# Delta attention on one core: the joins of neighbouring waves' inverses put side by side, and one transfer for their blocks

## What is computed

```python
mixed = (hidden_states @ W_qkvz).reshape(b, s, 16, 2*128 + 2*2*128)   # q, k, v, z of 16 key heads, 2 value heads each
qkv_c = silu(causal_conv4(q | k | v))
g = -exp(A_log) * softplus(a + dt_bias); beta = sigmoid(b_gate)
# by chunks of each value head
decay = exp(tril(g_cum_i - g_cum_j))
L = -(k * beta) @ k.T * decay, strictly lower
attn = solve_triangular(eye - L, eye, lower=True)                     # an inverse of a unit triangle
# the chain over a head's chunks
v_new = attn-solved v - attn-solved k @ state
out_i = (q * exp(g)) @ state + (q @ k.T * decay) @ v_new
state = state * exp(g_last) + (k * exp(g_last - g)).T @ v_new
# behind it
xf = core * silu(z); xf = xf * rsqrt(mean(xf * xf) + 1e-6) * norm_weight
out = xf @ W_out
```

## Time and profile before

| | |
|---|---|
| median of three executions | 2001.9 us |
| the profiled execution | 2008.92 us, span 2008.9 us |
| PE busy, loads of its weights | 1827.1 us (91%), 1171.5 us |
| DVE busy | 1353.0 us (67%) |
| ACT busy | 1041.1 us (52%) |
| POOL busy | 1018.1 us (51%) |

### The profile page before, as it was taken

How to read it: one execution, slowest core, us unless ns; L and a number is a source line. 1 busy time by engine, 2 the same in 40 slices (tenths; PEclk the granted TensorE clock), 3 DMA queues, 4 the chain that set the end, 5 groups by cost and what they waited for, 6 DMA issues and landing times.

```text
span 2008.9 us, 46738 instructions
## 1 busy us (share of the span) xinstructions
PE 1827.1 (91%) x16855; PEld 1171.5 (58%) x16855; DVE 1353.0 (67%) x2827; ACT 1041.1 (52%) x2817; POOL 1018.1 (51%) x2259
## 2 busy tenths in 40 slices
PE   7799997877799886898999999999999999999987
PEld 6422564432244565345677767776777677677766
DVE  2544464595669433636887888887778778888853
ACT  2466232224421342525666766766666677667653
POOL 0531122233100241124777877777777777777772
PEclk7899999897999796899999999999999999999988
DMA  5035423110010633202222222222222222222221
GB/s 138 21 98 176 105 46 54 55 65 1 1 45 0 172 117 102 35 20 51 53 51 63 62 47 63 65 53 54 65 65 55 54 65 65 55 54 65 49 41 32
DMA packets 231187, 124.48 MB, mean 62 GB/s; under 512 B 141360, under 2 KB 210512, under 8 KB 230704
## 3 DMA queue, kind: packets, MB, share of 16 engines
q1 hardware_dynamic: 225008, 111.20, 22.5%
q0 software_dynamic: 5952, 10.29, 2.3%
HBM read 87.94 MB, written 39.74 MB: 64 GB/s over the span
## 4 chain that ended last, share of the span: by engine, by line
PE 38%; DVE 6%; POOL 4%; ACT 4%; issue 3%; SPq 3%; DMA 2%; DVEq 0%; POOLq 0%; ACTq 0%
PE ps L2054 9%; PE ps L2064 4%; PE ps L2264 4%; PE ps L2231 3%; DVE a_qkv L2673 3%; PE ps L2240 2%; PE ps L2212 2%; PE ps L2295 2%; POOL a_z L2645 2%; POOL a_term L2641 2%; PE ps L2100 1%; SPq L1987 1%; PE ps L2199 1%; DVE a_low L2690 1%; PE ps L2251 1%
## 5 line engine op out<-in xcount | busy, mean ns | idle before, releaser
L2645 POOL TENSOR_TENSOR a_z<-a_z,a_term 32x14 f32<-32x14 f32 (+6 forms) x896 | 308.8, 345 | 70.2
L2641 POOL TENSOR_TENSOR a_term<-a_z,a_l 32x14 f32<-32x14 f32 (+6 forms) x896 | 296.1, 330 | 70.3
L2673 DVE SCALAR_TENSOR_TENSOR a_qkv<-a_raw,a_taps,a_qkv 128x512 f32<-128x512 f32 x384 | 277.3, 777 | 1.4
L2054 PE MATMUL ps<-all_xn,a_w_qkv 128*128 128x512 f32 x512 | 247.9, 610 | 0.0
L2264 PE MATMUL ps<-a_out_t,a_w_out 128*128 128x256 f32 x512 | 131.8, 402 | 6.3 <-ACT a_out_t L2510 5.7
L2408 ACT ACTIVATE a_raw<-ps 128x512 f32<-128x512 f32 x128 | 76.1, 596 | 108.7 <-PE ps L2054 108.6
L2635 POOL COPY a_z<-a_l 32x256 f32<-32x256 f32 x64 | 34.2, 535 | 189.9 <-DMA a_l<-a_v_dram 189.7
L2054 PEld LDWEIGHTS ps<-all_xn,a_w_qkv 128*128 128x128 f32 x512 | 89.4, 193 | 69.4 <-issue 67.5
L390 POOL DMA_INDIRECT f_rows<-a_row,a_slots x32 | 35.4, 1105 | 184.5 <-DVE a_of_tile L380 139.1
L2064 PE MATMUL ps<-a_w_z,all_xn 128*128 128x256 f32 x512 | 122.6, 383 | 0.0
L2264 PEld LDWEIGHTS ps<-a_out_t,a_w_out 128*128 128x128 f32 x512 | 94.7, 195 | 23.2 <-ACT a_out_t L2510 8.5
(11 more groups left out here) (343 smaller groups left out, 4417.0 us busy)
## 6 DMA issues: line engine op xcount, KB each, us to landing
a_gc_rows<-a_g_dram SPq DMA_DIRECT2D x64, 256.0 KB, 4.8
a_v_dram<-a_v SPq DMA_DIRECT2D x64, 256.0 KB, 2.1
a_w<-in_f_w SPq DMA_DIRECT2D x24, 512.0 KB, 4.4
a_w_qkv<-in_a_w SPq DMA_DIRECT2D x16, 512.0 KB
a_t_dram<-a_z SPq DMA_DIRECT2D x512, 8.0 KB
a_w_z<-in_a_w SPq DMA_DIRECT2D x16, 256.0 KB, 2.9
a_w_out<-in_a_wo SPq DMA_DIRECT2D x16, 256.0 KB, 3.1
a_v_off<-a_v SPq DMA_DIRECT2D x256, 4.0 KB
```

The lines of the kernel that those rows point to most:

```text
L2054: mm = pe.matmul(ps[:, to, :], w_qkv[:, k, mt * P:(mt + 1) * P], xn[:, k, b * T:(b + 1) * T], start=k == 0, stop=k == KC - 1)
L2641: pool.tensor_tensor(term[:, 0:j, j + 1:], z[:, 0:j, j:j + 1].broadcast_to([HP, j, n]), rows[:, j:j + 1, j + 1:].broadcast_to([HP, j, n]), ...
L2645: pool.tensor_tensor(z[:, 0:j, j + 1:], z[:, 0:j, j + 1:], term[:, 0:j, j + 1:], ALU.add).then_inc(sub_step, 1)
L2673: step = dve.scalar_tensor_tensor(to, rows, tap, to, ALU.mult, ALU.add)
```

## The change

1. **PE's order.** A round is now `join_a(w), close_b(w-1), make_scores(w+2), part 0, turn_keys(w+2), close_a(w), join_c(w-1), part 1, turn_out(w-2), join_b(w), close_c(w-1), recall(w-1)`, (c = 1: part 2), `project_out(w-2), solve(w-1)`, (c = 1: part 3, else part 2), `ask(w-1), grow_state(w-1), answer(w-1), turn_values(w+3)`; where c = 0, `turn_values` stands ahead of `ask`. The upper levels of wave w - 1 are now done in round w.
2. **The other engines' orders** follow: ACT's and DVE's loops are written anew, the exponents and `make_low` are made for w + 3 instead of w + 2 and `make_values` for w + 3, `widen` for w + 1. In the rounds c = 2 the convolutions go by batch (`conv_row`) between other steps. v0, v_far have a fourth buffer, `v0_off` two instead of three.
3. **SP.** The eight stores of a wave's inverted blocks become one of 32 partitions with 2 KB each; `z16` and `t_dram` are laid out for it, and the load that follows takes 128 bytes from four places for each partition. `spread` and `gather` are cut into five functions, whose order is the store of v0, the store of the blocks, the loads of `l16`, the load of the blocks, and the loads of `v0_off`.
4. **POOL** does `root(w-2), normed(w-2), substitute(w+2)`, which is the same order from wave to wave. `reduce` on DVE is gone: 1/128 goes into the scale of ACT's square, and the addition of 1e-6 is an instruction of POOL of 128x4 elements in `root`.
5. A constant tile `ident16` that nothing read is no longer loaded.

```diff
-                for w in range(-2, W + 1):
+                for w in range(-2, W + 2):
+                    if made(w - 2):
+                        root(w - 2)
+                        normed(w - 2)
                     if made(w + 2):
                         substitute(w + 2)
-                    if made(w - 1):
-                        root(w - 1)
-                        normed(w - 1)
...
                 def root(w):
-                    pool.wait_ge(var_ready, w + 1)
+                    pool.wait_ge(sq_ready, PR * (w + 1))
                     if w >= 1:
                         pool.wait_ge(xnorm_ready, w)
+                    pool.tensor_scalar(var[:, :], sums[:, :], 1e-6, None, ALU.add).then_inc(var_ready, 1)
+                    pool.wait_ge(var_ready, w + 1)
...
-                    if made(w + 3):
-                        load_gates(w + 3)
+                    if made(w + 4):
+                        load_gates(w + 4)
                     if made(w + 2):
-                        spread(w + 2)
+                        store_v0(w + 2)
                     if made(w + 1):
-                        gather(w + 1)
+                        store_t(w + 1)
+                    if made(w + 2):
+                        load_blocks(w + 2)
+                    if made(w + 1):
+                        load_t(w + 1)
+                    if made(w + 2):
+                        load_off(w + 2)
...
+                def store_t(w):
+                    sp.wait_ge(sub_done, w + 1)
+                    sp.dma_start(t_dram[w % 2].rearrange("(p x) -> p x", p=HP),
+                                 z16[:, w % 2, :, :, :].rearrange("p j k c -> p (j k c)")).then_inc(t_stored, 16)
...
                 for w in range(W + 2):
                     c, g = w % CH, w // CH + 1
                     silus = c == 1 and g < KH
                     if made(w - 1):
                         copy_half(w - 1)
                         copy_top(w - 1)
                         copy_far(w - 1)
                     if made(w - 2):
                         square(w - 2)
                     part(w, 0)
                     if made(w):
                         copy_tb(w)
                     if made(w - 1):
                         copy_wc(w - 1)
                     if silus:
                         silu(g, 0)
                     elif made(w + 2):
                         make_keys(w + 2)
                     if made(w - 2):
                         copy_out(w - 2)
                     if silus:
                         silu(g, 1)
                     if made(w):
                         copy_wb(w)
                     if made(w - 1):
                         copy_corners(w - 1)
                     part(w, 1)
                     if silus:
                         silu(g, 2)
                         part(w, 2)
                     else:
                         exponents(w + 3)
                     if made(w - 1):
                         new_values(w - 1)
                     if silus:
                         silu(g, 3)
                         part(w, 3)
                         exponents(w + 3)
                     else:
                         part(w, 2)
                     if made(w + 3):
                         make_values(w + 3)
```

More of the change, by code:

```diff
@@ L2344, in _ @@
                 f_lower(4)
+                turn_values(2)
                 for n in range(4):
@@ L2363, in _ @@
                 for w in range(W + 2):
[L2364 to L2374 removed]
+                    c = w % CH
                     if made(w):
@@ L2377, in _ @@
                     if made(w - 1):
-                        grow_state(w - 1)
+                        close_b(w - 1)
+                    if made(w + 2):
+                        make_scores(w + 2)
+                    part(w, 0)
+                    if made(w + 2):
+                        turn_keys(w + 2)
                     if made(w):
@@ L2381, in _ @@
                     if made(w - 1):
-                        answer(w - 1)
+                        join_c(w - 1)
+                    part(w, 1)
+                    if made(w - 2):
+                        turn_out(w - 2)
                     if made(w):
                         join_b(w)
-                    part(w, 1)
-                    if made(w):
-                        close_b(w)
-                    if made(w - 2):
-                        turn_out(w - 2)
-                    part(w, 2)
-                    if made(w + 2):
-                        turn_keys(w + 2)
-                    if made(w):
-                        join_c(w)
+                    if made(w - 1):
+                        close_c(w - 1)
+                        recall(w - 1)
+                    if c == 1:
+                        part(w, 2)
                     if made(w - 2):
                         project_out(w - 2)
-                    part(w, 3)
-                    if made(w):
-                        close_c(w)
+                    if made(w - 1):
+                        solve(w - 1)
+                    if c == 1:
+                        part(w, 3)
+                    else:
+                        part(w, 2)
+                    if c == 0 and made(w + 3):
+                        turn_values(w + 3)
+                    if made(w - 1):
+                        ask(w - 1)
+                        grow_state(w - 1)
+                        answer(w - 1)
+                    if c != 0 and made(w + 3):
+                        turn_values(w + 3)
             @block.scalar
@@ L2909, in _ @@
[L2909 to L2920 removed]
+                    if c == 2:
+                        conv_row(w, 1, 0)
+                    if made(w - 2):
+                        add_out(w - 2)
```

288 lines of the change are left out of this document (151 added, 137 removed).

## The result

| | before | after |
|---|---|---|
| median, us | 2004.9 (4 runs, 2001.8 to 2008.9) | 2134.6 (4 runs, 2124.0 to 2144.3) |
| ratio | 1 | **1.0635, 95% interval 1.0606 to 1.0663** |
| span of the profiled execution, us | 2008.9 | 2130.7 |
| granted clock, mean over the span | 0.952 | 0.918 |
| PE busy, us | 1827 | 1856 |

The change is slower by 6.3%, outside the range that was given.

What follows compares the result with a forecast made beforehand. PE was taken as the bound, with POOL next once PE gave 5%. PE's work, `turn_out` waits and ACT's delay summed to 67.35 us a head against 68.15, hence 1991 us against 2001.9; range 1964 to 2032.

Steps and rivals of the forecast that it cites:

- What the change takes off PE: On PE, fewer entries into and exits from tiled groups and small groups joined together: 2.5 us a head saved.
- The open term: On PE, eight changes from 32x32 to 64x64 tiles, shown by no row: between free and 0.19 us each.
- the lower bound: On PE, a full 0.19 us at each of the eight tile-size changes, leaving a saving of 1.0 us a head.
- The wait at c=1: PE at `turn_out` waits for POOL's xnorm about 3.4 us in each round c=1; 3.2 when carried from round to round.
- The chain: From v0 through store, block loads, `substitute`, `root` and `normed` on POOL: xnorm ready 20.6 us behind v0.
- The sum: Per head: PE's work 62.2, `turn_out` waits 4.7, ACT 0.65, small waits 0.2, less 0.4 on POOL: 67.35 us against 68.15.
- The wait at c=3: PE at `turn_out` waits for POOL's xnorm in round c=3: 1.2 us.
- The natural rounds: PE's rounds without the added waits: 16.2 us each, 13.6 for c=0, together 62.2 us a head.
- The clock: Rival: PE's long wait once a head brings half speed, 1.5 to 3.5 us a head; 2014 to 2042 us, chance 0.26.
- POOL doesn't hold PE: Rival: `substitute` runs faster or its waits are hidden; head 65.3 to 66.5 us, 1962 to 1979 us, chance 0.18.
- SP's limit of 16.3 us a wave: SP stores blocks before issuing the next loads, so `substitute` plus 3.2 us allows no wave under 16.3 us, no head under 65.3.
- ACT's backlog: ACT's work in round c=1 makes v0 about 1.4 us late in round c=2; counted as 0.65 us a head.

Runs made afterwards that it cites:

- the kernel without low clock: The changed kernel with part 1's matmuls repeated twice extra in rounds c=1 and once extra in rounds c=3: 2084.9 us, 1.0387 of the kernel before.
- the kernel with the block loads first: The changed kernel with SP's block loads issued ahead of the store of t: 2125.9 us, 1.0590 of the kernel before.
- the first filler: The changed kernel with part 1's matmuls run two extra times in every round c=1: 2084.3 us, 1.0364 of the kernel before.
- v0 first: The changed kernel with `make_v0` ahead of `copy_z_half` on DVE: 2107.2 us, 1.0493 of the kernel before.
- the filler of half the length: The changed kernel with part 1's matmuls run one extra time in every round c=1: 2116.5 us, 1.0524 of the kernel before.

## Why the prediction was wrong

*What the change takes off PE: right.* 2.5 us a head forecast within 1.0 and 3.4; 2.9 by the same kind of count, 2.5 by idle time. `join_a` with `close_b` takes 0.66 (1313.17 to 1313.83), as forecast. The open term, the change from 32x32 to 64x64 tiles, proved free: `close_a` with `join_c` takes 1.04 us to the next part (1316.82 to 1317.86), which is the 0.66 of 56 small records and 0.38 for `join_c`. So the lower bound, a full 0.19 at each of the eight places and 1.0 us a head, does not hold. The Trainium skill, TensorEngine Tiling (Array Packing), Key Properties, says that a change of the tiling mode drains TensorE: between two tiled modes no cost of it shows here, between the whole array and tiles it is the 0.09 and 0.10 us of the earlier trace rows.

*The wait at c=1: the mechanism right, its size near.* "PE waits about 3.4 us at `turn_out` in each round c=1": it does, and for what was named. The chain was put at 20.6 us behind v0 and took 21.3: the way to the first step of `substitute` 5.4 where 4.9 was taken, `root` with `normed` 3.1 where 2.55 was, `substitute` itself 12.9 where 13.1 was. In the kernel without low clock the rounds show waits of 4.1 us at c=1 (20.50 us a round, of which 3.5 are filler, less 16.40), as against the 3.2 of the sum. The 16.40 is round c=1 of the kernel with half the substitution, where `turn_out` waits for next to nothing; its rounds are 13.96, 16.40, 17.71 and 16.40 for c = 0 to 3.

*The sum: the step that failed.* It had PE's waits at `turn_out` too small, and the clock at nothing; the clock has its own paragraph below. Against the 67.35 us of the sum the head of 71.3 with hardly any low clock is 4 us longer, and two terms hold most of it. (1) The wait at c=3 was put at 1.2 and is 2.7 (19.11 less 16.40). That v0 of c=2 is late by 1.3 us was forecast; what was missing is that `substitute` begins 6.7 us behind it instead of 4.9. The loads of the blocks are issued 4.0 us behind v0 of c=2, where it is 2.3 behind v0 of c=0, and 3.8 and 2.4 in the kernel with the block loads first, so it isn't the store of t that they stand behind; what it is was not tested. (2) The wait at c=1, 0.9 too small; those of c=2, 0.45 too small (17.72 less 16.40, against 0.2 + 0.65). Together 2.9. The natural rounds were put at 62.2 and are 63.2 (13.96 and three times 16.40) with the small waits that stay in them, which the sum had beside them at 0.3, so 0.7 more; and the 0.4 us that POOL was to give back by quicker steps is already in the waits as measured, so it can't be taken off again. That makes 71.3, as it must, since the terms are the rounds of that kernel. With only these terms right, the forecast would have been a slowdown of 3 us a head, some 2%.

*The clock: put at nothing in the sum and among the rivals, and it came.* Its chance was 0.26, with "it decides from waits of about 3 us on" and 1.5 to 3.5 us a head. It cost 3.5 or more. The bound of 3 us was wrong, and it was the forecast's own sum that had PE wait 3.2 us a head: the forecast should have taken this case as its likeliest, on its own numbers. The gaps of the earlier trace rows, 3.09 us with the clock down and 0.82 with it up, said nothing of what lies between. The rival's 69 to 71 us a head fell short of 74.8 because its price stood on a sum that was 4 us too small.

*The other rivals.* That POOL doesn't hold PE fell. SP's limit of 16.3 us a wave did not bind: its repair changed nothing. ACT's backlog was there at 1.3 us for v0 in c=2, forecast 1.4.

*A cross-check that was to be had.* The change's order has only two parts and three small groups between the scores and `turn_out`, where `ask`, `solve`, `grow_state` and `answer` stood as well; the trace of before shows that `turn_out` was released by xnorm at c=1, with nothing to spare. Moved 5.4 us towards the scores (11.2 to 5.85), it must wait 5.4 us, less what the chain gains. That gain is 0.8 by the chain itself (22.1 to 21.3) and 0.8 by v0, which ends 2.3 us behind the scores of c=0 where it was 3.1, less 0.2 as round c=0 is that much shorter: 4.0 us, which is what the trace of the change has (9.8 less 5.85). It needs no sum over all rounds, and even twice the gain would have left a wait.

## What to carry to other kernels

Where work is reordered so that an engine's own stream gets shorter, measure for each consumer how long its input had been ready; a consumer moved nearer to a long chain on another engine loses that slack first. Here a whole round of distance, at the price of one more round at the loop's end, gave more than half of the substitution left out (1969.4 against 1979.9 us). A wait of some microseconds on TensorE, here from 1.6 us on, is to be priced twice, once as itself and once at the lower clock that can follow it; filling it with matmuls nobody needs showed how much is which.

## What the runs showed of the hardware

- Of the 28 waits of PE over 1 us in the changed kernel's loop, all 24 of 2.4 us or more had a stretch at the 1.2 GHz level begin in them or behind them, and two of the four of 1.56 us. Waits of nearly the same length went both ways in other kernels: of eleven of 1.56 us with the first filler seven brought a low stretch, of nine between 1.4 and 1.9 us in the kernel before with `turn_out` earlier three did, of eight of 1.88 us with v0 first all, and of eight of 1.6 us with the filler of half the length none. The length of the wait alone does not decide in this range.
- The low clock does not begin with the wait or end with it. In the changed kernel's loop it began between 2.3 us ahead of the wait's end and 2.1 us behind it: behind the 3.77 us wait, `turn_out` and the small tiles ran at full speed from 1455.94 to 1457.35, and then the part at half. The Trainium skill, TensorE: Matmul & The Clock Gate, HAM oscillation, has idle gaps between bursts of matmuls put the clock back each time. The trace agrees in part: it happened twice in nearly every head, in an engine that is busy for 91% of the stretch, but behind two of four waits of 1.56 us it did not. The page speaks of longer gaps than most of those here, and by the waits above shorter ones do it too.
- A change from 32x32 to 64x64 tiles inside one tiled stretch costs nothing that can be seen: `close_a` with `join_c` takes 1.04 us where apart they take 0.66 and 0.38.
